# Grouping TensorE's transposes: sixteen in a row over three banks, one bank for the down product

## The reference

```python
B_sel = B[adapter_ids]
A_sel = A[adapter_ids]
Bx = jnp.einsum('bni,bri->bnr', x, B_sel)      # "down": 1024 -> 16
out = jnp.einsum('bnr,bor->bno', Bx, A_sel)    # "up": 16 -> 1024
x = x + out * SCALING                          # SCALING is 1
```

## Time and profile before

| | |
|---|---|
| median of 3 runs | 92.24 us (92.05 to 92.42) |
| the profiled execution | 92.24 us, of which the span of the profile is 90.4 us |
| PE, PEld busy | 80.0 us (89%), 63.4 us (70%) |
| DVE, ACT, POOL busy | 59.5 us (66%), 59.1 us (65%), 60.6 us (67%) |
| moved by DMA | 34.82 MB, mean 385 GB/s |
| chain that ended last, by engine | PE 70%, DMA 14%, DVE 6% |
| granted TensorE clock, mean | 0.971 |

### The profile page before, as it was taken

One profiled execution on the slowest core, in us unless ns is written; L12 is line 12 of the kernel. 1 busy time (PEld: TensorE's weight loads), 2 busy tenths in 40 slices (PEclk: granted clock), 3 DMA queues, 4 the chain that ended last, 5 costly groups with the idle time before them and its releaser, 6 DMA issues.

```text
span 90.4 us, 3605 instructions
## 1 busy us (share of the span) xinstructions
PE 80.0 (89%) x1469; PEld 63.4 (70%) x1469; DVE 59.5 (66%) x106; ACT 59.1 (65%) x153; POOL 60.6 (67%) x136
## 2 busy tenths in 40 slices
PE   3999999999999999899999999999999999942600
PEld 3999997878686878577878786868787878720200
DVE  0039940319596959692949596959696969599950
ACT  2368498986868777659685968677786969450000
POOL 6000849999697969785969696979797978360000
PEclk9999999999999999999999999999999999999855
DMA  3899999999999999999999999999999999977695
GB/s 36 350 410 412 421 413 406 404 412 410 399 410 408 412 410 410 393 413 410 406 406 417 410 424 402 426 413 413 412 422 408 421 397 415 373 303 317 259 404 223
DMA packets 8945, 34.82 MB, mean 385 GB/s; under 512 B 482, under 2 KB 482, under 8 KB 8930
## 3 DMA queue, kind: packets, MB, share of 16 engines
q1 hardware_dynamic: 8784, 34.08, 94.2%
q10 hardware_dynamic: 146, 0.52, 1.5%
HBM read 17.83 MB, written 16.78 MB: 383 GB/s over the span
## 4 chain that ended last, share of the span: by engine, by line
PE 70%; DMA 14%; DVE 6%; SPq 2%; DVEq 1%; issue 1%; ACT 1%
PE t_bank L221 32%; PE y_banks L252 19%; PE bx_bank L232 19%; DMA x_all<-in_x 14%; DVE x_all L365 4%; DVE bx_parts L356 2%; SPq L135 2%; DVEq L49 1%; ACT bx_parts L287 1%; SPq L131 0%
## 5 line engine op out<-in xcount | busy, mean ns | idle before, releaser
L365 DVE TENSOR_TENSOR x_all<-y_banks,x_all 128x1024 f32<-128x1024 f32 x32 | 39.3, 1230 | 15.9 <-PE y_banks L252 15.3
L305 ACT COPY x_t<-t_bank 128x512 f32<-128x512 f32 x64 | 34.5, 592 | 14.5 <-PE t_bank L221 13.9
L171 POOL CAST a_duo<-a_table 128x512 fp32r x64 | 36.8, 619 | 3.5 <-PE y_banks L252 2.2
L221 PE MATMUL t_bank<-ident,x_all 128*128 128x128 f32 x256 | 34.8, 279 | 0.2 <-DMA x_all<-in_x 0.2
L161 POOL COPY b_duo<-b_table 128x256 f32 x64 | 22.9, 403 | 15.8 <-PE bx_bank L232 8.7
L221 PEld LDWEIGHTS t_bank<-ident,x_all 128*128 128x128 f32 x256 | 27.6, 141 | 7.3 <-issue 5.5
L252 PE MATMUL y_banks<-a_duo,bx_parts 64*128 64x512 f32 x128 | 20.1, 421 | 3.7 <-ACT bx_parts L287 3.2
L232 PE MATMUL bx_bank<-x_t,b_duo 128*32 128x64 f32 x1024 | 21.2, 222 | 0.0
L232 PEld LDWEIGHTS bx_bank<-x_t,b_duo 128*32 128x32 f32 x1024 | 16.1, 109 | 5.5 <-issue 5.4
L356 DVE TENSOR_TENSOR bx_parts<-bx_bank,bx_parts 32x64 fp32r<-32x64 f32 x64 | 14.1, 220 | 4.8 <-ACT bx_parts L320 3.7
L252 PEld LDWEIGHTS y_banks<-a_duo,bx_parts 64*128 64x128 f32 x128 | 10.7, 184 | 7.2 <-issue 3.8
(11 more groups left out here) (10 smaller groups left out, 5.4 us busy)
## 6 DMA issues: line engine op xcount, KB each, us to landing
x_all<-in_x SPq DMA_DIRECT2D x6, 2048.0 KB, 22.2
out_y<-x_all SPq DMA_DIRECT2D x3, 2048.0 KB, 20.9
out_y<-x_all SPq DMA_DIRECT2D x6, 1024.0 KB, 10.5
out_y<-x_all SPq DMA_DIRECT2D x8, 512.0 KB, 3.8
x_all<-in_x SPq DMA_DIRECT2D x3, 1024.0 KB, 20.9
x_all<-in_x SPq DMA_DIRECT2D x2, 512.0 KB, 6.2
x_all<-in_B ACTq DMA_DIRECT2D x1, 512.0 KB, 4.8
x_all<-in_A SPq DMA_DIRECT2D x1, 512.0 KB, 4.6
```

What stands on the lines that cost most here:

```text
L171: last = nc.gpsimd.tensor_copy(a_duo[duo % 2][:, k, :], a_table[:, bass.ds(adapters[k] * BANK, BANK)])
L221: last = nc.tensor.transpose(t_bank[unit % 2][:, c * P:(c + 1) * P], x_all[:, 2 * duo + tile, at:at + P], ident[:, :])
L305: nc.scalar.copy(x_t[duo % 2][:, half * HALF:(half + 1) * HALF, tile, :], t_bank[unit % 2][:, :].rearrange("p (c n) -> p c n", c=HALF)).th ...
L365: nc.vector.tensor_tensor(here, product, here, ALU.add).then_inc(y_drained, 1)
```

## The change

Three edits.

1. **Banks.** `t_bank` gets a third bank, `bx_bank` keeps one of its two. All duos' down products go to this one bank. A transpose unit takes bank n % 3, n being the unit's running number, and waits until the unit three before it was copied. The second half of B's transposes at the start goes to the third `t_bank`. The first half of D(duo) has a new wait: `rest_done`, that VectorE has read the down product of the duo before.
2. **Order of TensorE.** For each duo: all four units of T(duo+1), first half of D(duo), U(duo-1), second half of D(duo). U stays out of the loop's middle for duo 0 and for duo 15; U(14) and U(15) follow the loop. The orders of ScalarE, VectorE and GpSimd are as they were.
3. **Loads.** Tiles 4 to 7 come in two loads of two tiles (1 MB each) and no longer in one of four.

```diff
+    T_BANKS = 3
...
-    LOADS = [(0, 1), (1, 2), (2, 4)] + [(t, t + 4) for t in range(4, 24, 4)] + [(24, 26), (26, 30), (30, 32)]
+    LOADS = [(0, 1), (1, 2), (2, 4), (4, 6), (6, 8)] + [(t, t + 4) for t in range(8, 24, 4)]
+    LOADS += [(24, 26), (26, 30), (30, 32)]
...
-        t_bank = [pb(f"t_bank{i}", [P, BANK]) for i in range(2)]
-        bx_bank = [pb(f"bx_bank{i}", [P, BANK]) for i in range(2)]
+        t_bank = [pb(f"t_bank{i}", [P, BANK]) for i in range(T_BANKS)]
+        bx_bank = pb("bx_bank", [P, BANK])
+        b_banks = [bx_bank, t_bank[T_BANKS - 1]]
...
-                if duo or unit >= 2:
-                    pe.wait_ge(t_copied, B_UNITS + UNITS * duo + unit - 1)
+                n = UNITS * duo + unit
+                if n >= T_BANKS - 1:
+                    pe.wait_ge(t_copied, B_UNITS + n - (T_BANKS - 1))
...
-                    last = nc.tensor.transpose(t_bank[unit % 2][:, c * P:(c + 1) * P],
+                    last = nc.tensor.transpose(t_bank[n % T_BANKS][:, c * P:(c + 1) * P],
...
             def down(duo, first, end):
                 if first == 0:
                     pe.wait_ge(b_gathered, duo + 1)
+                    if duo:
+                        pe.wait_ge(rest_done, duo)
...
-                        last = nc.tensor.matmul(bx_bank[duo % 2][k * QUAD:(k + 1) * QUAD, 0:SEQ],
+                        last = nc.tensor.matmul(bx_bank[k * QUAD:(k + 1) * QUAD, 0:SEQ],
...
                 if duo + 1 < DUOS:
-                    transpose_unit(duo + 1, 0)
-                    transpose_unit(duo + 1, 1)
+                    for unit in range(UNITS):
+                        transpose_unit(duo + 1, unit)
                 down(duo, 0, HALF)
-                if duo + 1 < DUOS:
-                    transpose_unit(duo + 1, 2)
-                    transpose_unit(duo + 1, 3)
+                if 0 < duo < DUOS - 1:
+                    up(duo - 1)
                 down(duo, HALF, CHUNKS)
-                if duo:
-                    up(duo - 1)
+            up(DUOS - 2)
             up(DUOS - 1)
```

More of the change, by code:

```diff
@@ L196, in _ @@
                 for c in range(HALF):
-                    last = nc.tensor.transpose(bx_bank[unit][:, c * P:(c + 1) * P],
+                    last = nc.tensor.transpose(b_banks[unit][:, c * P:(c + 1) * P],
                                                b_nat[:, (unit * HALF + c) * P:(unit * HALF + c + 1) * P], ident[:, :])
@@ L299, in _ @@
                     [:, unit * HALF:(unit + 1) * HALF],
-                    bx_bank[unit][:, :].rearrange("p (c a r) -> p c a r", c=HALF, a=ADAPTERS)).then_inc(t_copied, 1)
+                    b_banks[unit][:, :].rearrange("p (c a r) -> p c a r", c=HALF, a=ADAPTERS)).then_inc(t_copied, 1)
             def copy_x(duo, unit):
@@ L305, in copy_x @@
                 nc.scalar.copy(x_t[duo % 2][:, half * HALF:(half + 1) * HALF, tile, :],
-                               t_bank[unit % 2][:, :].rearrange("p (c n) -> p c n", c=HALF)).then_inc(t_copied, 1)
+                               t_bank[(UNITS * duo + unit) % T_BANKS][:, :].rearrange("p (c n) -> p c n", c=HALF)).then_inc(t_copied, 1)
             def copy_a(a):
@@ L320, in split_high @@
                     last = nc.scalar.copy(bx_parts[duo % 2][0:QUAD, k, s * SEQ:(s + 1) * SEQ],
-                                          bx_bank[duo % 2][k * QUAD:(k + 1) * QUAD, 0:SEQ])
+                                          bx_bank[k * QUAD:(k + 1) * QUAD, 0:SEQ])
                 last.then_inc(high_done, 1)
@@ L356, in split_rest @@
                     last = nc.vector.tensor_tensor(bx_parts[duo % 2][QUAD:K_UP, k, cols],
-                                                   bx_bank[duo % 2][k * QUAD:(k + 1) * QUAD, 0:SEQ],
+                                                   bx_bank[k * QUAD:(k + 1) * QUAD, 0:SEQ],
                                                    bx_parts[duo % 2][0:QUAD, k, cols], ALU.subtract)
```

## The result

The changed kernel takes 99.0 us in the median of six runs (98.12 to 100.79), against 92.29 for the kernel before (92.05 to 92.89). Two of the six runs (100.15 and 100.79) are over 1.5% above the fastest, and the ratio leaves them out: 1.068 (95% interval 1.064 to 1.072). The forecast was 95.8, at most 97.4. The direction and the stall that carried it were right; the size was not.

The account below looks back on a forecast made before the run. TensorE's stream was taken as the bound. D(0)'s end 15.7, 14 periods of 4.56 (63.8), irregular gaps 1.2, tail 9.9 and last store 3.4 give span 94.0; with 1.84 outside it 95.8 us, range 94.2 to 97.4.

Parts of the forecast that it names:

- The stall at the fourth unit: In each duo's transposes, the fourth unit waits for ScalarE's copy 0 behind split_high: starts at 1.68, not 1.31, stall 0.37 us.
- Sixteen transposes in a row: In TensorE's stream, joining both halves of the transposes takes 1.89 us, not 2.04: 0.15 saved per duo without waits.
- One down bank, covered by the copy's stall: Down's wait for split_rest of the duo before is seen at 2.01; the stall puts down at 2.28 anyway.
- I keep 1.2 us: Irregular "issue" gaps of TensorE over the whole run: 1.2 us, taken over unchanged from the kernel before.
- The loads: At the start, T(2)'s wait for tiles 4 to 7 goes: 0.3 us gained; the added DMA start costs nothing.
- The tail: From D(14)'s end to VectorE's last add: 9.9 us, 0.9 longer because D(15) and U(14) stand behind the new wait.
- Rival A: Copy 0 is seen before about 1.4 after D's end, so no stall: 92.2 or 90.5 us; chance 0.09.
- Rival B: The DMA backlog until 77 us hides the slower stream behind the stores: no change, 92.2 us; chance 0.04.
- Rival C: TensorE's clock swings to its lower level in three duos of fourteen: +3 to +13, taken as 100 us; chance 0.07.

Follow-up runs that it names:

- e3: Changed kernel with the up product put back behind both halves of down; sixteen transposes, three transpose banks and one down bank stay; 97.69 us, ratio 1.054.
- e13: e12 plus a wait on rest_done of the duo before in down's first half, not needed with its two down banks; 96.3 us, ratio 1.041.
- e2: Changed kernel with the old loads; 98.94 us, ratio 1.061.
- e4: Changed kernel without the loads of tiles 8 to 31, later tiles reading tile number modulo 8; 93.97 us, ratio 1.013.
- e1: Kernel before with only the new loads (tiles 4 to 7 in two loads); 92.61 us, ratio 1.000.
- e15: e13 without the loads of tiles 8 to 31, later tiles reading tile number modulo 8; 95.14 us, ratio 1.027.
- e12: Kernel before with VectorE's split_rest placed before the first add of the duo before; 92.48 us, ratio 1.000.
- e14: e13 with the added wait on a semaphore that has had its value since the start; 92.78 us, ratio 1.002.
- e9: e3 with VectorE's split_rest placed before the first add of the duo before; 96.11 us, ratio 1.044.
- e10: Kernel before, own banks and loads, with only the up product moved between the second pair of transpose units and down's second half; 94.17 us, ratio 1.023.
- e5: Kernel before without the loads of tiles 8 to 31, later tiles reading tile number modulo 8; 91.77 us, ratio 0.989.
- e6: Kernel before's TensorE order with the change's banks, loads and waits; 104.7 us, ratio 1.132.

## Why the prediction was right and wrong

- **The stall at the fourth unit: right.** Seen at 1.65 (forecast 1.68), period 4.53 (4.56). e3, without it, has 4.08.
- **Sixteen transposes in a row: right.** In e3 they take 27.83 - 25.92 = 1.91 (forecast 1.89). At the start both halves of down stand together and take 1.03, as in e3 (28.88 - 27.83 = 1.05), not 1.17; that, with a start 0.3 us earlier, is why D(0) ended at 15.29.
- **One down bank, covered by the copy's stall: right for the period, wrong for the whole.** The bank is read 0.3 us before down. Only who waits how long was priced. In e13 the same wait, with nothing to protect, brings 2.7 us of irregular time at an unchanged period, in gaps at the places where instruction blocks begin. No run takes it out of the changed kernel, so its part there is argued.
- **"I keep 1.2 us": the step that failed.** It was 5.9 in the profile of the changed kernel and 4.8 in e2. The one row of it was called irregular and carried over without asking what ended it, and the range let the term only shrink (-1.2 to 0). What the runs show in its place: waits for late instruction blocks, four gaps of 4.03 us in sum in the changed kernel (3.76 in e2), where the kernel before has one of 0.39. With 12.6 MB of loads left out the term is 0.7 (e4).
- **The loads:** the wait at the start went as forecast, and the end didn't notice (e1).
- **The tail:** 10.5 us for 9.9. D(15) waited for split_rest(14) as said; the up products after it ran at the lower clock (granted 0.51 from 87.7 us on): from their first matmul to the add it takes 1.13 (87.68 to 88.81) in place of 0.77.
- **Rival A** (in time, faster) had its deciding point at 1.4 and the copy was seen at 1.65. **Rival B** (hidden by the stores) is excluded: the DMA share is 0.66 from 68 to 84 us, and the time grew. **Rival C** (clock) is a small part, about 1.1 us of one execution (5.9 against e2's 4.8). Its price had a wrong reading: the 1.50 of the earlier trace rows was not at the lower clock, which begins at 85.21 in that trace; the second tile's weight loads waited for VectorE's add there (81.19, 0.47). After the gap of 1.93 the records of up cover 2.02 us, in the changed kernel:

```profile
28.52 0.71 PE L225 MATMUL t_bank<-ident,x_all 128*128 128x128 f32 x5 [1.93 <-issue]
...
29.74 2.02 PE L258 MATMUL y_banks<-a_duo,bx_parts 64*128 64x512 f32 x8
```

and 1.20, the usual value, in e2 after the same gap:

```profile
28.81 0.71 PE L224 MATMUL t_bank<-ident,x_all 128*128 128x128 f32 x5 [1.93 <-issue]
...
30.03 1.20 PE L257 MATMUL y_banks<-a_duo,bx_parts 64*128 64x512 f32 x8
```

The regular stalls of 0.33 to 0.36 us, ten of them, left the granted clock at 1.00 from 36 to 84 us. So the rule of the Trainium skill, page "TensorE: Matmul & The Clock Gate", section "A second HAM failure mode: psum-queue depth-cycling", which expects small idles between groups to make the clock swing, did not hold for these stalls; of the four longest irregular gaps, three were followed by the lower level within 1.5 us (1.93 in the changed kernel, 1.64 in e3, 2.03 in e15), and 1.93 in e2 was not.

**What stays open.** Shown: the gaps are waits for instruction blocks (43 of 43, by time and by place); blocks start later when the DMA engines are full (103 to 105 instructions ahead against 182); in e4 the gaps nearly vanish with 12.6 MB of loads; in the old order the wait on rest_done makes most of them at an unchanged period (e13 against e12 and e14), and it holds the sequencer for some 1.77 us a group. Only argued: that a held sequencer asks for its next block later, and that this is what sets the changed kernel apart from the kernel before, whose blocks start as far ahead on average but more evenly. e9 and e10, which give and take room at other waits, do not fit a simple form of this. That e3's large gaps come from its pace, 4.08 us for as many instructions, is argued too. No version here beats the kernel before.

## What to carry to other kernels

Copy chains have to be counted in the written order of the engine that copies: a third bank bought nothing here, because its copy stood behind work that the moved up product had been hiding. Where an engine's stream is long, unrolled and nearly full while the DMA engines are full too, its instruction blocks are one more transfer that can be late; look up what ends each "issue" gap, and count whether the gaps lie multiples of the same number of instructions apart, before carrying them over as noise. A semaphore wait that the matmuls never feel isn't free for such an engine: read how long the sequencer stands at it, and price it by a run with the same wait on a semaphore long fulfilled beside it.

## What the runs showed of the hardware

- A wait that is fulfilled 0.1 us before its matmul's turn, but holds TensorE's sequencer for some 1.77 us in 14 of 15 groups, cost 3.8 us, 0.8 of it direct (e13); the same wait long fulfilled cost 0.3 or less (e14, 92.78 against 92.48).
- All 43 irregular gaps of TensorE, 0.16 to 2.03 us long, ended 2.2 to 2.7 us after the start of a 16 KB transfer on the instruction queue, and stood multiples of 256 instructions apart.
- With few loads these transfers started 182 instructions ahead of their place on average (e4, e5), with all loads 103 to 105 (the kernels before and after).
- Both halves of down in one row take 1.05 us for 64 matmuls, 0.12 less than in two halves.
- These profiles put a wait for another engine under "issue" where an instruction carries several waits (the 0.83 us of e6, the 1.97 at the changed kernel's end): a regular "issue" is read from the timeline, by who ends just before.
